# A two-layer graph attention on one core: K alone in the projection stage, Q, V and skip beside the scores, node blocks ordered by size

## What is computed

```python
for l in range(2):
    q = (x @ Wq[l] + bq[l]).reshape(N, H, D)
    k = (x @ Wk[l] + bk[l]).reshape(N, H, D)
    v = (x @ Wv[l] + bv[l]).reshape(N, H, D)
    a = (q[dst] * k[src]).sum(-1) * scale
    e = exp(a - segment_max(a, dst)[dst])
    alpha = e / (segment_sum(e, dst)[dst] + 1e-16)
    agg = segment_sum(alpha[:, :, None] * v[src], dst).reshape(N, C)
    x = agg + (x @ Ws[l] + bs[l]) + enc
x = layer_norm(x); x = relu(x @ W1 + b1) @ W2 + b2 + x
out = layernorm(enc + layer_norm(x) + enc)
```

## Time and profile before

| | |
|---|---|
| median of 3 runs | 2437.12 us (2436.15 to 2437.2) |
| profiled execution, own time | 2427.93 us |
| its span | 2426.2 us |
| busy in the span | PE 1935.8, DVE 1813.3, POOL 1677.3, ACT 1457.2 us |
| stages, layer 0 | tables to 42, project to 183, score to 638, collect to 1095 us |
| stages, layer 1 | project to 1243, score to 1697, collect to 2152 us |

### The profile page before, as it was taken

How to read it: one execution, slowest core, us unless ns; L and a number is a source line. 1 busy time by engine, 2 the same in 40 slices (tenths; PEclk the granted TensorE clock), 3 DMA queues, 4 the chain that set the end, 5 groups by cost and what they waited for, 6 DMA issues and landing times. The chain is left out here.

```text
span 2426.2 us, 47903 instructions
## 1 busy us (share of the span) xinstructions
PE 1935.8 (80%) x8220; PEld 1313.4 (54%) x8221; DVE 1813.3 (75%) x2465; ACT 1457.2 (60%) x8263; POOL 1677.3 (69%) x1660
## 2 busy tenths in 40 slices
PE   2987888888389888877969888886498888859997
PEld 2873444444167555555844444442385555547876
DVE  5526878788798777775748777888897777778994
ACT  1325878787487666662238777787596666643222
POOL 2667777777667777764767777776677777747663
PEclk8997999999789999998989999999699999989999
DMA  2558989998667777766769999997677777761201
GB/s 91 209 194 315 300 300 297 300 301 284 184 191 210 209 211 209 210 196 227 262 253 300 299 300 300 301 300 217 186 210 211 210 210 210 210 214 53 70 35 50
DMA packets 188287, 536.02 MB, mean 221 GB/s; under 512 B 36132, under 2 KB 36516, under 8 KB 188136
## 3 DMA queue, kind: packets, MB, share of 16 engines
q0 software_dynamic: 116512, 381.77, 51.8%
q1 hardware_dynamic: 62984, 137.09, 16.0%
q10 hardware_dynamic: 8640, 15.73, 2.0%
HBM read 465.99 MB, written 68.17 MB: 220 GB/s over the span
## 5 line engine op out<-in xcount | busy, mean ns | idle before, releaser
L663 POOL DMA_INDIRECT score_rows<-k_rows,score_index x704 | 679.2, 965 | 216.2 <-issue 187.8
L663 POOL DMA_INDIRECT coll_rows<-v_rows,coll_index x704 | 667.9, 949 | 226.5 <-issue 205.4
L1030 PE MATMUL coll_banks<-coll_ev,coll_hot 128*128 128x260 f32 x2816 | 689.9, 393 | 131.4 <-DVE all_work L1102 112.4
L902 ACT ACTIVATE all_work<-all_work 128x64 f32<-128x64 f32 x2752 | 660.2, 241 | 196.9 <-DVE all_work L825 165.2
L1030 PEld LDWEIGHTS coll_banks<-coll_ev,coll_hot 128*128 128x128 f32 x2816 | 515.5, 190 | 305.7 <-DVE all_work L1102 231.8
L1165 ACT ACTIVATE coll_ev<-coll_rows,graph_edge 128x64 f32<-128x64 f32 x2112 | 542.5, 335 | 229.5 <-DMA coll_rows<-v_rows,coll_index 229.3
L782 PE MATMUL score_q_ps<-layer_q,all_work 128*128 x2112 | 530.6, 388 | 165.8 <-DVE all_work L825 138.8
L825 DVE TENSOR_TENSOR all_work<-score_q_ps,score_rows 128x1024 f32<-128x1024 f32 x352 | 429.0, 1219 | 160.9 <-DMA score_rows<-k_rows,score_index 118.5
L902 ACT ACTIVATION_READ_ACCUMULATOR all_work<-all_work (+1 forms) x2752 | 513.7, 187 | 0.0
L782 PEld LDWEIGHTS score_q_ps<-layer_q,all_work 128*128 128x128 bf16 x2112 | 192.7, 99 | 450.7 <-issue 301.3
L1090 DVE TENSOR_TENSOR coll_ev<-coll_rows,coll_banks 128x640 f32<-128x640 f32 x352 | 287.9, 818 | 135.0 <-DMA coll_rows<-v_rows,coll_index 131.0
(11 more groups left out here) (220 smaller groups left out, 2366.3 us busy)
## 6 DMA issues: line engine op xcount, KB each, us to landing
all_work<-local_dst SPq DMA_DIRECT2D x44, 512.0 KB, 7.9
x_turned<-proj_xt SPq DMA_DIRECT2D x40, 512.0 KB, 2.7
score_xt<-x_turned SPq DMA_DIRECT2D x40, 512.0 KB, 6.3
score_rows<-k_rows,score_index POOLq DMA_INDIRECT x704, 4.9
coll_rows<-v_rows,coll_index POOLq DMA_INDIRECT x704, 3.7
skip_rows<-proj_base POOLq DMA_DIRECT2D x40, 256.0 KB, 3.2
k_rows<-proj_k_out SPq DMA_DIRECT2D x40, 256.0 KB, 2.0
all_work<-skip_rows SPq DMA_DIRECT2D x40, 256.0 KB, 6.3
```

The lines of the kernel that those rows point to most:

```text
L663: nc.gpsimd.indirect_dma_start(rows[:, slot, t, :], None, table, at).then_inc(arrived[slot], 16)
L902: last = nc.scalar.activation(at, at, ACT.Copy, accum_out=k.edge[:, bass.ds(n * TPS + t, 1), h:h + 1].rearrange("p a b -> p (a b)"))
L1030: last = nc.tensor.matmul(sums[s % SUMS][:, part, :], m, ev[:, s % EVS, t, part * AGG // 2:(part + 1) * AGG // 2], start=t == 0, stop=t == ...
```

## The change

- `project` becomes `keys`: only K is computed there, with two buffers and static loops. In layer 0 it also splits all eight weight matrices of both layers (Wk, Wq, Wv, Ws) and stores six of them split in DRAM (`k.w_d`); later stages load the split halves by SP. Q's weights of the layer stay in SBUF (`k.wq`). The biases of Q, V and skip become two rows (high and low) and are added by a 13th matmul with two rows of contraction.
- `score` computes Q, V and skip of one block per half: 39 matmuls, 5 after each step (`PER_STEP`). Q is taken as two fp32r parts, high by ACT, low by DVE, so a step has 4 fp32r matmuls in place of 6 bf16. V is taken by ACT, skip by DVE. The base of the skip rows is x itself, loaded by SP into one buffer (two before).
- The blocks are ordered by their number of steps, largest first, since the Q of the block at place i must be there when its first step comes. `order_row` and `place_row` hold the order; SP and PE read their addresses from them.
- The one-hot matrices are fp32r, made for 2 steps at a time (`PAIR`, 4 per half), with loads of row numbers of 1 KB per partition in place of 4 KB.
- The product buffers of `score` are 2 in place of 4 (`PRODS`); gathered K rows lie in `k.work`.
- The marks of segment starts go to DRAM and are loaded in each `soften_collect`. `score` ends with `give_back` (semaphores cleared, one more barrier).

```diff
-PRODS = 4
+PRODS = 2
-Q_PARTS = 3
+PAIR = HOT_STEPS * SE
+OUTS = 3
+SIDE = 3 * KC + 1
+PER_STEP = -(-OUTS * SIDE // HALF)
```

In `build_step_tables`, the places of the blocks:

```diff
+                link(v.scalar_tensor_tensor(rank[:], n_steps[:], float(P), numbers, ALU.mult, ALU.subtract))
+                link(v.tensor_tensor(before[:], rank[:].unsqueeze(1).to_broadcast([P, BLOCKS, BLOCKS]),
+                                     rank[:].unsqueeze(2).to_broadcast([P, BLOCKS, BLOCKS]), ALU.is_gt))
...
+def keys(nc, k, layer):
```

In `keys`, the loop of SP:

```diff
+                for b in range(BLOCKS):
+                    u = b % 2
+                    if b + 2 < BLOCKS:
+                        load(b + 2)
...
+                    sp.wait_ge(lo_ready, b + 1)
+                    sp.dma_start(k.xt_d[b * P:(b + 1) * P, :], xt[:, u].rearrange("p a c n -> p (a c n)").bitcast(F32)
+                                 ).then_inc(xt_stored[u], 16)
+                    sp.wait_ge(out_done, b + 1)
+                    sp.dma_start(k.k_d[b * P:(b + 1) * P, :], k_out[:, u, :]).then_inc(k_stored[u], 16)
+                    if first and b == BLOCKS // 2:
+                        sp.wait_ge(fresh_known, 1)
+                        sp.dma_start(k.fresh_d, fresh[:]).then_inc(fresh_out, 16)
```

In `keys`, POOL in layer 0:

```diff
+                    load(0)
+                    load(1)
+                    for i in range(2, n):
+                        load(i)
+                        if i >= 3:
+                            store_split(i - 1)
+                    store_split(n - 1)
```

In `keys`, ACT:

```diff
+                for b in range(2, BLOCKS):
+                    high_part(b)
+                    if first and b - 2 < QUARTS:
+                        copy_keys(b - 2)
+                    elif first and b % 2 == 0 and b // 2 - 2 < len(matrices):
+                        weight_high(b // 2 - 2)
```

In `keys`, DVE:

```diff
+                for b in range(BLOCKS):
+                    if b + 1 < BLOCKS:
+                        low_part(b + 1)
+                    if not first and b + 2 < BLOCKS:
+                        assemble(b + 2)
+                    take_keys(b)
...
+                    if first and b % 2 == 0 and 2 <= b // 2 - 2 < len(matrices):
+                        weight_low(b // 2 - 2)
```

In `score`, SP (the row numbers of a pair of steps, one half, the start):

```diff
+                def locals_of(half, slots):
+                    for i in slots:
+                        sp.wait_ge(hot_ready, PAIRS * half + i + 1)
+                        load_local(PAIRS * half + i + 2, i % 2)
+
+                def run_half(half, q, skip_before, place, next_place, now_base):
+                    locals_of(half, (0,))
+                    if skip_before is not None:
+                        store_skip(half, skip_before)
+                    locals_of(half, (1,))
+                    if now_base:
+                        node = first_node(place)
+                        sp.wait_ge(skip_stored, 16 * half)
+                        load_base(node)
+                    if next_place is not None:
+                        node = first_node(next_place)
+                        sp.wait_ge(skip_product, half)
+                        load_xt(node, q)
+                    locals_of(half, (2, 3))
+                    if place is not None:
+                        node = first_node(place)
+                        sp.wait_ge(v_done, half + 2)
+                        sp.dma_start(k.v_d[bass.ds(node, P), :], v_out[:]).then_inc(v_stored, 16)
+
+                load_xt(first_node(0), 0)
+                load_local(0, 0)
+                load_local(1, 1)
+                for part in range(2):
+                    sp.dma_start(w_v[part][:].rearrange("p c n -> p (c n)").bitcast(F32), k.w_d[layer, 2, part]).then_inc(v_in, 16)
+                load_xt(first_node(1), 1)
+                for part in range(2):
+                    sp.dma_start(w_skip[part][:].rearrange("p c n -> p (c n)").bitcast(F32), k.w_d[layer, 3, part]).then_inc(s_in, 16)
+                load_base(first_node(1))
+                locals_of(0, (0, 1))
```

In `score`, PE:

```diff
                             for t in range(TPS):
+                                e = (s % HOT_STEPS * TPS + t) * P
+                                for part in range(2):
+                                    last = nc.tensor.matmul(q_ps[s % 2][:, t, :], hot[:, s // HOT_STEPS % 2, e:e + P],
+                                                            parts[:, part * C:(part + 1) * C], start=part == 0, stop=part == 1)
                             last.then_inc(q_ready, 1)
+                            for i in range(s * PER_STEP, (s + 1) * PER_STEP):
```

In `score`, DVE, one half:

```diff
                         for s in range(HALF):
                             multiply(n + s, s, half + 1)
+                            if s % HOT_STEPS == 0 and not (ends and s == HALF - HOT_STEPS):
+                                ahead = s // HOT_STEPS + 1
+                                one_hot(PAIRS * half + ahead, ahead % 2, PAIRS // 2 * half + ahead // 2 + 1)
                             if s > 0:
                                 add_up(n + s - 1, s - 1, heads)
+                            if s == 1 and sides[h][0]:
+                                take_skip(half)
+                            if s == 4 and sides[h][1]:
+                                q_low(half + 1)
```

In `score`, ACT:

```diff
+                        if s % HALF == 3 and sides[s // HALF][0]:
+                            q_hi(half + 1)
+                        if s % HALF == 6 and sides[s // HALF][1]:
+                            take_v(half)
```

In `soften_collect`, SP and DVE:

```diff
+                sp.dma_start(fresh[:], k.fresh_d).then_inc(fresh_in, 16)
...
                 dve.wait_ge(turned, 1)
+                dve.wait_ge(fresh_in, 16)
                 link(scan(fwd[:], before, big[:, 0:SLOTS], -BIG))
```

More of the change, by code:

```diff
@@ L61 @@
 EPS = 1e-5
-assert STEPS % BODY == 0 and TILES % CHUNKS == 0 and STEPS + HALF <= TABLE and 2 * KC == HALF
+assert STEPS % BODY == 0 and TILES % CHUNKS == 0 and STEPS + HALF <= TABLE
+Q_BY = 6
+assert all(i * EDGE_ROWS > BLOCKS * (HALF * (i - 1) + Q_BY - 1) for i in range(1, BLOCKS))
 class Shared:
@@ L241, in _ @@
+                link(v.tensor_tensor(before[:], before[:], numbers.unsqueeze(1).to_broadcast([P, BLOCKS, BLOCKS]), ALU.mult))
+                link(v.tensor_reduce(order[:], before[:], AX.X, ALU.add))
+                link(v.tensor_copy(k.order_row[:], order[0:1, :]))
                 dve.wait_ge(src_in, 16 * STEP_GROUPS)
@@ L557, in _, with low_rows @@
-                link = chain(dve, marks) if layer == 0 else None
-                v = nc.vector
+                    dve.wait_ge(x_in[u], 16 * (b // 2 + 1))
+                    v.tensor_tensor(x[:, u, :], x[:, u, :], skip[:, u, :], ALU.add).then_inc(x_ready, 1)
+                def low_rows():
+                    dve.wait_ge(rows_hi, 1)
+                    for i in range(len(bias_rows)):
+                        at = slice(32 * i, 32 * i + 1)
+                        last = v.tensor_tensor(rows_lo[at, :], rows_raw[at, :], k.bias[at, :].bitcast(F32), ALU.subtract)
+                    last.then_inc(rows_split, 1)
@@ L866, in body @@
+                q_low(0)
+                def body(it, sides, heads, last):
+                    for h in range(2):
+                        half = 2 * it + h
+                        n = BODY * it + HALF * h
+                        ends = last and h == 1
                         for s in range(HALF):
                             multiply(n + s, s, half + 1)
-                            if s == 0 and (with_blocks or q == 0):
-                                nc.vector.tensor_copy(index[:, 1 - q, :], sources[:, bass.ds((half + 1) * HALF * TPS, HALF * TPS)]
+                            if s == 0 and not ends:
+                                nc.vector.tensor_copy(index[:, 1 - h, :], sources[:, bass.ds((half + 1) * HALF * TPS, HALF * TPS)]
```

760 lines of the change are left out of this document (387 added, 373 removed).

## The result

The changed kernel takes 2443.23 us (median of 20 runs, 2433.18 to 2452.91), the kernel before, on the same chip, 2436.32 us (20 runs): ratio 1.0027, 95% interval 1.0015 to 1.0039. It is slower by a quarter of a per cent; faster was forecast, at 2426 us. The time lies inside the stated range of 2400 to 2462 us. The profiled span is 2437.0 us, 10.8 more than before.

A forecast was written before the change was run, and what follows sets the result against it. Gather issue bounds score and collect, PE the projections. Terms -32 - 3 + 1.3 + 2 + 2.6 + 11.6 + 6.6 = -10.9 us take the profiled 2427.9 to 2417.0; the median's 9.2 more gives 2426, range 2400 to 2462.

The forecast's parts named there:

- The score loop through SP: Score, per half: skip store, three loads, one-hot to skip take 19.2 to 19.7 us against 20.0, so cost zero.
- rival B: Score stages: the SP loop decides, at 20.9 us a half costs 34 us, giving 2460 us; chance 0.22.
- One-hots, plus 11.6: Score stages: 88 short one-hots per layer hold gathers 10.2 us in place of 4.4, plus 11.6 for both layers.
- hand-over: End of score: giving semaphores back costs 1 us each time, plus 2 us in all.
- Start of the score stage: Late row numbers of pair 2 cost 3.3 us a layer, less 2.0 for splits gone: plus 2.6 for both.
- K alone, layer 1: Layer 1's K stage: a loop of 4.9 us per block makes it 32 us shorter, bounds minus 22 and minus 37.
- K alone, layer 0: Layer 0's K stage, with all weight splits: DMA traffic leaves minus 3 us, bounds minus 12 and plus 12.
- Segment starts, plus 6.6: Start of collect: loading the segment starts delays the first scan by 3.3 us per layer, 6.6 in all.

The follow-up runs named there:

- e1b: The changed kernel with SP loading the row numbers of pair 4 ahead of the skip base and the turned block: 2406.80 us, ratio 0.9890.
- e6c: e1b with layer 1's Q, V and skip matrices split in layer 1's K stage, low parts on GpSimd, two blocks of skip rows loaded first: 2413.87 us, ratio 0.9920.
- e8c: e1b with four product buffers in place of two and the low part of the skip matrix left out: 2398.72 us, ratio 0.9854.
- e9c: e6c with the second turned block ahead of V's weights and pair 2's row numbers ahead of the skip weights in score: 2411.51 us, ratio 0.9905.
- e10: e1b with layer 0's K stage splitting the stored matrices after blocks 2 to 12 in place of 8 to 18: 2401.47 us, ratio 0.9865.
- e11: e10 with e9c's score start order; in layer 1's K stage skip rows ahead of K's weights, Q's weights behind blocks 4 and 7: 2402.64 us, ratio 0.9864.
- e2b: The changed kernel with ACT's loop over two halves in the score stage written out: 2445.45 us, ratio 1.0045.
- e1: The same kernel as e1b, run in a session where the kernel before takes 3049 us: ratio 0.9996.

## Why the prediction was wrong, point by point

- **The score loop through SP, "Zero, by a hair": this is the step that failed.** The mechanism was named right and one term was too small. The three loads I put at 7.4 us, scaled from landings of two other sizes; from the first issue to the one-hot they take 8.8. In the half shown 1.7 us of that pass before the last load is issued (448.27 to 449.98), where the kernel before had 1.1 between its three issues; the block order is looked up in between. The rest held: store to next issue 4.1 (said 4.2), one-hot to store 7.8 (said 7.5 to 8.0). The sum is 20.7 in place of 19.2 to 19.7 (my own terms add up to 19.1 to 19.6). It lies over the 20.0 of the gathers, and the rounds' averages, 0.75 and 0.62 us over it, make 26 us in 38 rounds. Taking the loop out by the order of one load gave 30.2 us back (e1b): shown. So rival B's mechanism was right, for which I had used the same term at its upper bound, and which I gave 0.22; its 34 us were too many.
- **One-hots, plus 11.6: too dear.** In e1b the gathers that are themselves long (over 0.97 us) lose 4.4 and 4.5 us per layer; before, they lost 6.9 and 5.6, some 2.0 of it by the splits. 88 short one-hots cost about as much as 22 long ones. In the other variants with the row numbers first (e6c, e8c, e9c, e10, e11) the loss is 2.2 to 3.8 us a layer. The score stages of e1b, ends included, are 4.4 us longer than before in both layers, against 16.2 forecast for start, one-hots and hand-over. That is why B did not end at its 2460 us. The Trainium skill ("SBUF — State Buffer", Who interferes with whom) has a tensor_scalar in a two-port mode and GpSimd hold each other for a whole instruction; if the one-hots run in such a mode, 88 of 0.48 us, 42 us in all, beside gathers that come every 1.25 us lose 4.4 us here, so the trace does not agree in size.
- **Start of the score stage.** Forecast +3.3 a layer for the late row numbers; the one stall is 2.8 and 4.3 us in e1b, and goes when the row numbers and the second turned block are moved forward (e11): right in size.
- **K alone, layer 1, minus 32:** right, -35.6 with the hand-over, and -31 to -34 in the other traces of the same code. The first K sum starts 18.4 us after DVE's first operation of the stage (1120.5 to 1138.9; 18 said), and 19 blocks take 90.3 us, 4.75 each (4.9 said).
- **K alone, layer 0, minus 3 with bounds of 12:** the mechanism was right (the DMA share is 0.94 on average from 104 to 184 us), the end was not. The sum of the bytes holds: from the K sum of block 8 to 188 us pass 29.7 MB at 338 GB/s (30.8 said, 80 to 88 us). But that sum starts at 100.3 us, not at 93: the first K sum comes at 62.5, and one of the first eight blocks takes 9.1 us in place of 4.2, ACT waiting 7.5 us for a turned block's store. How the bytes lie matters too: the last matrix is split at block 18, and its 2 MB hold the stage 7 us beyond the last K row; e10 removes that tail with the same bytes. First gather +6.0 against -1.7.
- **Segment starts, plus 6.6:** +1.7 on the collect stages. In layer 0 the first scan starts 5.5 us after the first gather (5.05 before), in layer 1 4.9 (4.7 before). The load lands 6.2 us after its issue in layer 1, where I had 9.7 from the start of the stage, about when the matmuls end that the scan waits for anyway.
- **The end, not forecast:** +4.1 us, in code that the change does not touch (below).

Stretch by stretch the trace differs from the forecast by +30.2 (the loop, by e1b), -11.8 (one-hots, start and hand-over), +7.7 (first stage), -3.6 (K of layer 1), -4.9 (segment starts) and +4.1 (the end): 21.7 us in all. The median stands 4.4 us above the profiled execution's own time, where I had taken the 9.2 of the kernel before, and that makes the 17 us between 2426 and 2443. That the miss is only 17 us is in part luck: the loop alone is 30, and the one-hots, reckoned too dear, took some of it back.

## What to carry to other kernels

A loop whose sum comes within a few per cent of the bound that should hide it is not hidden: give it the upper bound of its worst-known term, or take a transfer out of it, before work is moved in. Put the small load that an in-order engine needs next ahead of the large ones that it needs later; one line of order was worth 30 us here, and by the spans of the traces it turned a change that costs 11 us into one that saves 20. And don't take a DMA share of 0.6 for free room in a stage that is a chain of transfers: here 10 to 23 us went with the splits moved into it, in part by other causes.

## What the hardware did that I had not expected

- The finish after the last gather of collect 1 takes 287.4 to 289.0 us in nine traced executions of the changed kernel and its variants, 284.3 in a tenth (e6c), and 283.3 before. Its code is the same in all. Timeline of DVE and GpSimd where it arises, of the changed kernel and then of e6c:

```profile
2304.56 11.46 DVE L1470 SCALAR_TENSOR_TENSOR mlp_y<-mlp_y,mlp_y_scale,mlp_shift 128x512 f32<-128x512 f32 x4
...
2306.42 4.05 POOL L1396 TENSOR_TENSOR mlp_enc<-mlp_enc 128x2048 f32<-128x2048 f32 x1
2310.54 4.93 POOL L1398 TENSOR_TENSOR mlp_enc<-mlp_enc,mlp_shift 128x2048 f32<-128x2048 f32 x1
```

```profile
2281.30 7.11 DVE L1487 SCALAR_TENSOR_TENSOR mlp_y<-mlp_y,mlp_y_scale,mlp_shift 128x512 f32<-128x512 f32 x4
...
2283.81 4.05 POOL L1413 TENSOR_TENSOR mlp_enc<-mlp_enc 128x2048 f32<-128x2048 f32 x1
2287.94 4.95 POOL L1415 TENSOR_TENSOR mlp_enc<-mlp_enc,mlp_shift 128x2048 f32<-128x2048 f32 x1
```

  Four DVE operations take 11.5 us where GpSimd's two come 1.9 us behind their start, and end 0.55 us after the second of these; where GpSimd comes 2.5 us behind they take 7.1 and end 0.55 us after the first, as they do before. In all eleven traces the group ends 0.55 us after one of GpSimd's two operations, and the nine in which it is the second are the nine with the long finish. So 4.4 us hang on an arrival 0.65 us earlier. The Trainium skill (same section) says that a DVE instruction with two operands in SBUF contends with GpSimd's reads and that the later one is blocked; the trace agrees in kind, and so do the two held adds in e6c's K stage above. No run moved this alignment on purpose.
- ACT pauses 3 to 4 us in most rounds of its loop (256 operations a round); written out, it doesn't (e2b). The pause was there before the change too (six waits of up to 3.6 us in score 0). Taking it out of the changed kernel gained nothing; out of the kernel before it was not taken.
- In three of the sessions the kernel before takes 25 to 27% longer than in the others. By e1 and e1b the operations of ACT, DVE and GpSimd are as long there (188 and 187 ns, 1.22 and 1.22 us, 0.95 and 0.95 us in the mean) and pauses lie between them; PE's are longer too (448 and 393 ns for those of collect), with granted clocks of 0.83 and 0.93 in the mean.
